# Image 0 of a four-block convolution chain: x loaded once, late weights spread over the gathers, and fewer spacer instructions between the gathers

## The reference, cut to what matters

```
L0: mid = relu(bn(conv1x1(x, 512->128)))
    offset = conv3x3(mid, 128->18)
    samp = for each of 9 taps: 4 neighbouring pixels of mid at (pixel + tap + offset),
           weighted bilinearly
    hid = relu(bn(sum over taps of conv2_w[tap] @ samp[tap]))
    x = relu(bn(conv1x1(hid, 128->512)) + x)
L1: 25 local self-correlations of x, normalised; x = relu(W @ [x, corr] + b)
L2, L3: x = relu(bn(1x1, 3x3, 1x1 bottleneck of x) + x)
```

## Time and profile before

| | |
|---|---|
| median of 3 runs | 602.6 us |
| profiled execution: its own time, its span | 605.4 us, 603.6 us |
| busy: TensorE, VectorE, ScalarE, GpSimd | 562.2, 442.3, 327.3, 409.5 us |
| first gather of image 0, of image 1, last of image 3 | 24.9, 129.2, 471.7 us |
| moved by DMA | 110.1 MB |

### The profile page before, as it was taken

The page is one execution under the profiler, slowest core; times in us unless marked ns, Lnnn a source line. Parts: engine busy times, 40 slices in busy tenths (PEclk is TensorE's granted clock), DMA queues, the critical chain, the costliest instruction groups (busy, mean ns, idle before and its releaser), DMA issues.

```text
span 603.6 us, 8850 instructions
## 1 busy us (share of the span) xinstructions
PE 562.2 (93%) x2550; PEld 416.9 (69%) x2550; DVE 442.3 (73%) x1277; ACT 327.3 (54%) x718; POOL 409.5 (68%) x718
## 2 busy tenths in 40 slices
PE   9478986699999999799999999999999999999996
PEld 4434753576777777469777777688777776987774
DVE  3447789798988788689986788998884674463444
ACT  3445756446654874555645857654557633433534
POOL 2388888888888898888888888888787300003060
PEclk9888998899999999899999999999999999999999
DMA  8898997964568555866586557856765213000003
GB/s 307 286 355 292 276 366 222 310 186 143 160 193 296 165 150 162 280 205 171 168 264 204 168 168 251 251 159 175 223 183 148 72 59 134 0 1 1 1 1 139
DMA packets 48034, 110.08 MB, mean 182 GB/s; under 512 B 7655, under 2 KB 15911, under 8 KB 47858
## 3 DMA queue, kind: packets, MB, share of 16 engines
q0 software_dynamic: 23040, 75.52, 41.8%
q1 hardware_dynamic: 22274, 32.59, 15.6%
q10 hardware_dynamic: 2672, 1.41, 0.8%
HBM read 96.94 MB, written 12.55 MB: 181 GB/s over the span
## 4 chain that ended last, share of the span: by engine, by line
PE 71%; POOL 18%; DVE 4%; issue 3%; DMA 2%; ACT 1%; POOLq 0%; DVEq 0%; ACTq 0%
PE bank L630 16%; PE bank L632 16%; PE bank L631 16%; POOL patch L597 14%; PE bank L741 7%; POOL tick L602 4%; PE bank L749 4%; PE bank L818 4%; PE bank L730 4%; DMA patch<-patch_tables,idx_all 2%; PE bank L787 1%; PE bank L666 1%; PE bank L653 1%; DVE samp L1189 1%; DVE ring L1250 1%
## 5 line engine op out<-in xcount | busy, mean ns | idle before, releaser
L1189 DVE SCALAR_TENSOR_TENSOR samp<-patch,wgt_all,samp 128x128 f32<-128x128 f32 x864 | 240.7, 347 | 22.7 <-ACT samp L911 20.1
L597 POOL DMA_INDIRECT patch<-patch_tables,idx_all x216 | 219.8, 1017 | 40.2 <-DVE samp L1189 10.7
L911 ACT ACTIVATE samp<-patch,wgt_all 128x128 f32<-128x128 f32 x288 | 102.0, 396 | 76.4 <-DMA patch<-patch_table,idx_all 35.3
L597 POOL DMA_INDIRECT patch<-patch_table,idx_all x72 | 70.5, 980 | 30.9 <-DVE far L1086 20.3
L613 POOL TENSOR_TENSOR kept<-xs_high,xs_low 128x512 f32<-128x512 f32 x12 | 16.5, 1405 | 100.3 <-PE bank L632 100.3
L602 POOL TENSOR_TENSOR tick<-tick 1x1 f32<-1x1 f32 x288 | 79.7, 277 | 5.0
L741 PE MATMUL bank<-sampT,w 128*128 128x512 f32 x144 | 71.9, 606 | 1.5 <-ACT sampT L919 1.5
L730 PEld LDWEIGHTS bank<-ident_r,samp 128*128 128x128 f32 x288 | 35.8, 144 | 31.4 <-DVE samp L1189 16.8
L919 ACT ACTIVATE sampT<-bank 128x512 f32<-128x512 f32 x72 | 41.9, 591 | 27.8 <-PE bank L730 26.8
L730 PE MATMUL bank<-ident_r,samp 128*128 128x128 f32 x288 | 44.1, 280 | 10.5 <-DVE samp L1189 10.5
L630 PE MATMUL bank<-x_high,l1w_high 128*128 128x512 f32 x128 | 53.9, 421 | 0.0
(11 more groups left out here) (187 smaller groups left out, 1203.1 us busy)
## 6 DMA issues: line engine op xcount, KB each, us to landing
x_whole<-in_x SPq DMA_DIRECT2D x32, 256.0 KB, 7.2
out_y<-ring SPq DMA_DIRECT2D x32, 256.0 KB, 3.3
xa<-in_x SPq DMA_DIRECT2D x6, 1024.0 KB, 8.5
patch<-patch_tables,idx_all POOLq DMA_INDIRECT x216, 3.5
patch_tables<-midT SPq DMA_DIRECT2D x11, 256.0 KB, 7.1
xa<-in_x SPq DMA_DIRECT2D x8, 256.0 KB, 5.7
patch<-patch_table,idx_all POOLq DMA_INDIRECT x72, 6.0
l1w_whole<-in_l1wt SPq DMA_DIRECT2D x1, 1024.0 KB, 10.4
```

The source lines that it names most:

```text
L597: pool.indirect_dma_start(patch[:, n % SLOTS].rearrange("p a c -> p (a c)"), None, patches_n if i else patches_0, bass.IndirectOffsetOnAxi ...
L911: act.activation(samp[:, n % SAMPS, t, :], patch[:, g % SLOTS, 0, :], ACT.Copy, scale=wgt_all[:, i, (HT * h + t) * TAPS + k, 0:1]).then_in ...
L1189: dve.scalar_tensor_tensor(o_, g_, w_, o_, ALU.mult, ALU.add).then_inc(blended, 1)
```

## The change

The list is planned anew: all engines' items stand in another order (the bulk of the diff, not shown). What was counted in it for this document stands in the prediction. Nine items are gone (`xload.1.0` and all eight `res.0`), ten `ldw` items (loads of weights) are new. The code outside the list:

```diff
-PAUSE, PAUSES = 120, 2
+PAUSE, PAUSES = 120, (0, 1, 2, 2)
+WEIGHT_PACE = {7: 1, 2: 2, 3: 2, 4: 3, 5: 3, 0: 4, 1: 4, 6: 7}
+X_PACE = {2: 0, 3: 5}
...
             def load_x(i, h):
-                sp.dma_start(xa[:, :, h * HALF:(h + 1) * HALF],
-                             x_v[i, :, :, h * HALF:(h + 1) * HALF]).then_inc(ld_xa[h], 16)
-
+                some = slice(h * KC // 2, (h + 1) * KC // 2)
+                sp.dma_start(xa[:, some, :], x_v[i, :, some, :]).then_inc(ld_xa[h], 16)
+
+            for k in range(KC):
+                sp.dma_start(whole["x1"][:, k, PADK:PADK + H, :], grid_rows(x_v[0, :, k, :])).then_inc(ld_x0[k], 16)
             for h in range(2):
-                for k in range(KC):
-                    cols = slice(h * HALF, (h + 1) * HALF)
-                    sp.dma_start(xa[:, k, cols], x_v[0, :, k, cols]).then_inc(ld_x0[h][k], 16)
-            for n in (2, 3, 4, 5, 6, 0, 1):
...
-            sp.wait_ge(tabled[0], table_dmas(0))
-            sp.wait_ge(conv1_done, nth(("conv1", 0, 1)))
-            load_x(1, 1)
...
+                load_x(1, h)
 
             for it in ORDER:
                 if it[0] == "xload":
                     _, i, h = it
-                    sp.wait_ge(conv1_done, nth(("conv1", i - 1, h)))
+                    sp.wait_ge(conv1_done, nth(("conv1", i - 1, 0), ("conv1", i - 1, 1)))
+                    sp.wait_ge(turned, nth(("turn", 0, X_PACE[i] + h)))
                     load_x(i, h)
+                elif it[0] == "ldw":
+                    n = it[1]
+                    if n in WEIGHT_PACE:
+                        sp.wait_ge(turned, nth(("turn", 0, WEIGHT_PACE[n])))
+                    else:
+                        sp.wait_ge(tabled[0], table_dmas(0))
...
                                 .then_inc(gathered[n % SLOTS], 16)
+                        if i == 0 and t % 2 == 0:
+                            continue
                         pool.wait_ge(ticked, ticks[0] + 1)
                         pool.tensor_tensor(tick[:, 1:2], tick[:, 0:1], tick[:, 0:1], ALU.add).then_inc(ticked, 1)
                         ticks[0] += 1
-                        for _ in range(PAUSES if i and t == HT - 1 else 0):
+                        for _ in range(PAUSES[i] if t == HT - 1 else 0):
...
-            for _ in range(3):
-                pe.matmul(bank[TURN_BANK][:], w3_s[:, 0:P], w3_s[:], start=True, stop=True)
-            pe.wait_ge(ld_first, 32)
+            for n in (C, C // 2):
+                pe.matmul(bank[TURN_BANK][:, 0:n], w3_s[:, 0:P], w3_s[:, 0:n], start=True, stop=True)
+            pe.wait_ge(ld_w1, 16)
...
+                        elif h == 0:
+                            pe.wait_ge(ld_x0[c], 16)
+                            for half in range(2 if c < KC - 1 else 1):
+                                last = pe.matmul(first[half][:], w1[:, c, :], residual(half, c),
+                                                 start=c == 0, stop=c == KC - 1)
```

More of the change, by code:

```diff
@@ L50 @@
[L50 to L74, removed]
@@ new lines @@
+weigh.0.4.0 tap.0.1 turn.0.3 ldw.4 gather.0.5.1 conv1.2.1 midT.1.0 ldw.5 weigh.0.4.1 blend.0.4.0 gather.0.6.0
+blend.0.4.1 conv1.2.0 hats.1 gather.0.6.1 weigh.0.5.0 blend.0.5.0 weigh.0.5.1 gather.0.7.0 sampT.0.3 mid.2.1 turn.0.4
+midT.2.1 split.3 weigh.0.6.0 blend.0.5.1 positions.1 splitlow.3 ldw.0 gather.0.7.1 ldw.1 weigh.0.6.1 mid.2.0
+pixels.1.0 blend.0.6.0 turn.0.5 tap.0.2 tap.0.3 midT.2.0 split.5 blend.0.6.1 gather.0.8.0 xload.3.0 pixels.2.0
+weigh.0.7.0 taps.2.1 tapped.2.1 sampT.0.4 weigh.0.7.1 sampT.0.5 gather.0.8.1 splitlow.5 blend.0.7.0 blend.0.7.1
@@ new lines @@
+gather.0.12.1 blend.0.11.0 hid.0.0 weigh.0.11.1 split.4 out0.0.0.0 out0.0.0.2 gather.0.13.0 out0.0.0.3 splitlow.1
+blend.0.11.1 gather.0.13.1 split.6 sampT.0.9 weigh.0.12.0 turn.0.10 out0.0.0.1 turn.0.11 xsum.0.0.2 blend.0.12.0
+conv1.3.1 weigh.0.12.1 xhigh.0.0.2 mid.3.0 gather.0.14.0 xsum.0.0.1 weigh.0.13.0 gather.0.14.1 xhigh.0.0.1 corrw
+xsum.0.0.3 splitlow.4 gather.0.15.0 xhigh.0.0.3 sampT.0.11 xsum.0.0.0 xlow.0.0.2 blend.0.12.1 xlow.0.0.1 blend.0.13.0
+mid.3.1 weigh.0.13.1 weigh.0.14.0 sampT.0.10 tap.0.9 tap.0.10 turn.0.12 midT.3.1 taps.3.0 gather.0.15.1 weigh.0.14.1
@@ new lines @@
+turn.0.16 sampT.0.15 blend.0.17.1 sampT.0.16 gather.1.1.0 weigh.1.0.0 turn.0.17 tap.0.15 sampT.0.17 tap.0.16
+gather.1.1.1 tap.0.17 splitlow.6 index.3 hid.0.1 weigh.1.0.1 gather.1.2.0 blend.1.0.0 out0.0.1.2 out0.0.1.3
+blend.1.0.1 out0.0.1.0 out0.0.1.1 gather.1.2.1 turn.1.0 xsum.0.1.2 hats.3 positions.3 xsum.0.1.3 xhigh.0.1.2
+weigh.1.1.0 weigh.1.1.1 xhigh.0.1.3 gather.1.3.0 xlow.0.1.2 xsum.0.1.1 xsum.0.1.0 xhigh.0.1.1 mixA.0.0.0 mixA.0.0.1
+xlow.0.1.3 xhigh.0.1.0 weigh.1.2.0 xlow.0.1.1 borders xlow.0.1.0 blend.1.1.0 gram.0.1 gather.1.3.1 weigh.1.2.1
@@ new lines @@
+weigh.3.3.1 hid.2.1 xsum.2.0.1 blend.3.3.0 gather.3.5.1 turn.3.2 turn.3.1 final.1.1.1 xhigh.2.0.1 sampT.3.2
+blend.3.3.1 store.1.1.1 weigh.3.4.0 xlow.2.0.1 out0.2.1.3 out0.2.1.0 gather.3.6.0 blend.3.4.0 sampT.3.1 weigh.3.4.1
+tap.3.0 out0.2.1.1 mixA.2.0.0 tap.3.1 tap.3.2 out0.2.1.2 blend.3.4.1 gather.3.6.1 turn.3.3 xsum.2.1.1 xsum.2.1.3
+xsum.2.1.0 xhigh.2.1.3 xhigh.2.1.0 xlow.2.1.3 turn.3.4 gram.2.0 xlow.2.1.0 gather.3.7.0 xsum.2.1.2 weigh.3.5.0
+xhigh.2.1.1 xhigh.2.1.2 weigh.3.5.1 xlow.2.1.1 weigh.3.6.0 xlow.2.1.2 gather.3.7.1 blend.3.5.0 gram.2.1 copies.2.0
```

365 lines of the change are left out of this document (186 added, 179 removed).

## The result

The changed kernel takes **610.4 us** in the median of 4 runs (608.6 to 611.1), the kernel before on the same chip 603.0 (602.5 to 605.9): a ratio of **1.0116, 95% interval 1.0081 to 1.0151**. The forecast was 597.6 with a range of 590.5 to 604.5. It is slower, by 7.4 us, where a gain of 5 was foreseen. The profiled execution of the change (608.6) is its fastest, that of the kernel before (605.4) one of its slower ones, so the two traces lie only 3.2 us apart in span; they show how the parts moved, the ratios say how much it came to.

What follows compares the result with a forecast made beforehand. The prediction saw a start, a stretch at POOL's pace (image 0's gathers), then one at TensorE's. Its terms, -1.0 - 11.7 + 1 + 5.7 + 3 - 2 = -5.0, took 602.6 to 597.6 us, range 590.5 to 604.5.

Steps and rivals of the forecast that it cites:

- Term 1: First stage: halved warm-up and no parameter wait bring the first gather earlier, -1.0 us (bounds -2.5 to +1.0).
- Term 2: POOL in image 0: 36 dropped ticks save 0.325 us a pair, -11.7 us.
- rival B: POOL in image 0: a gather directly behind a gather pays what the tick paid; 608.3 us, chance 0.15.
- Term 3: Faster stretch at POOL's pace: VectorE, TensorE and DMA nearly full, so lumps cost +1 us (0 to +6).
- rival D: First stretch: VectorE or transfers full, POOL waits for slots, half the tick gain lost; 602.3 us, chance 0.20.
- Term 4: TensorE: two mixA move behind image 0's last tap, 2.85 us each, +5.7 us.
- term 5: VectorE behind image 0's last blend: splitlow.6, index.3, positions.3 delay xsum and xlow for gram, +3 us (0 to +6.2).
- term 6: TensorE's wait at 230 to 260 us for image 1's last gathers shrinks, -2 us (0 to -4.2).

Runs made afterwards that it cites:

- u3_pause: The change with two memsets per four gathers in image 1 again, not one; 614.17 us, ratio 1.0167.
- v1_rest: Kernel before, its list and early weights kept, with most other edits of the change (ticks, single x load, halved warm-up, conv1's start, pauses); 596.65 us, ratio 0.9878.
- d1_ticks: Kernel before without the tick behind the first gather of each pair of image 0; 602.67 us, ratio 0.9988.
- d2_xonce: Kernel before with image 0's x loaded once, into the residual's place, in the same eight pieces; 603.10 us, ratio 0.9993.
- d3_noticks: Kernel before with no tick at all in image 0; 598.67 us, ratio 0.9910.
- o2_mixA: The change with index.3, hats.3, positions.3, borders, splitlow.6 and two mixA moved back near their old places in its list; 616.74 us, ratio 1.0219.
- o1_borders: The change with index.3, hats.3, positions.3 and borders moved up in its list; 654.6 us, ratio 1.0439, on a slower chip.
- u2b_ticks: The change with a tick again behind every gather of image 0; 610.98 us, ratio 1.0113.
- h3_mixA: v1_rest with two mixA moved behind tap.0.17, image 0's last tap; 652.4 us, ratio 1.0342, on a slower chip.

## Why the prediction was wrong

**Term 1, the first gather, -1.0 (bounds -2.5 to +1.0).** Measured +0.8 in the change's trace and -2.1 in u3_pause's, from the same code; v1_rest, with the same warm-up, lies between (conv1's 14 pieces in 7.40, the first gather at 23.82). In two microseconds of that stretch, the change and u3_pause:
```profile
9.00:11.00 2.00, 2.00 (x4) 0.74 (x3) 1.21 (x7) 0.23 (x2) 0.00 (x0) 1.00 1.02 418
```
```profile
9.00:11.00 2.00, 2.00 (x6) 0.85 (x5) 1.21 (x7) 0.21 (x2) 0.00 (x0) 1.00 1.02 420
```
TensorE is busy throughout in both, with four pieces begun in the one and six in the other, and the granted clock reads 1.00, the level of 2.4 GHz, in both. It reads 1.00 from 1.47 to 5.00 in the trace of before too, where the warm-up's pieces take 0.92 us each and conv1's later 0.47, so at the start of the kernel this column does not tell the two paces apart. The bounds held; the single value hid that the outcome varies. What decides it stays open.

**Term 2, the ticks, -11.7.** This is the step that failed: "if the second gather starts 0.01 behind the first as the tick does now". It starts 0.30 behind. The tick's 0.18 and 0.16 are exchanged for a gap of 0.30, so a pair saves 0.06 us and not 0.325, 2.2 us over 36 pairs, and d1_ticks shows that even this does not arrive. It is rival B's mechanism, just short of its bound: by B there is nothing to win from a second gather of 1.30 us on, and it takes 1.24, 0.30 to start and 0.94. B's "against", that each tick starts at once behind its gather, was no evidence on a gather; the idle 0.16 behind each tick should have told me that a gather has a start of its own to pay.

The sum's other half, that the excess over the shortest step is inherited and not saved, was right in kind; its size varies. Over the 71 steps it is 9.4 us before, 12 us in d1_ticks, 7.6 us in the change's trace (mean step less half of the shortest pair, times 71). It stands beside VectorE's subtractions of two SBUF operands. In the change a tick lasts 2.12 us from 131.11 on, beside `splitlow.6`:
```profile
131.11 2.12 POOL L613 TENSOR_TENSOR tick<-tick 1x1 f32<-1x1 f32 x1
```
```profile
130.90 2.28 DVE L1185 TENSOR_TENSOR l1w_low<-l1w_whole,l1w_high 128x2048 fp32r<-128x2048 f32 x1
```
In v1_rest it is a second gather itself, with no tick ahead of it, that lasts 2.54 where others last 0.95, beside two such subtractions:
```profile
47.09 2.54 POOL L596 DMA_INDIRECT patch<-patch_table,idx_all  x1 [0.30 <-issue]
```
```profile
46.86 1.35 DVE L1175 TENSOR_TENSOR l2w_low<-l2w_whole,l2w_high 128x1152 fp32r<-128x1152 f32 x1
48.12 0.68 DVE L1175 TENSOR_TENSOR l3w_low<-l3w_whole,l3w_high 128x512 fp32r<-128x512 f32 x1
```
The Trainium skill's rule on two SBUF inputs (SBUF — State Buffer, Who interferes with whom) had been set against the change in just this form, and this trace agrees with it for the gather too: the gather begins 0.23 us after the first subtraction and ends 0.83 us after the second. The same section infers that such a subtraction does not hold up the writing of a transfer's descriptors; the 2.54 us of this indirect transfer speak against that. In the prediction's own pair the agreement is less clean than it says: the tick begins at 78.47, 0.05 ahead of the subtraction, so by the starts it was the earlier one that waited.

**Term 3, +1.** The stretch at POOL's pace got 3.9 us shorter, where terms 2 and 3 together said 10.7. In image 0 POOL does not wait for slots; rival D did not happen. The bytes were right: 282 GB/s in 108.6 us are 30.6 MB, 30.1 had been worked out, though the text says half of image 1's x where its 2.1 MB are the whole.

**Term 4, two `mixA`, +5.7.** The work behind the last tap grew by 5.0 us and 24 pieces: right in the two traces, with the 2 us of doubt on the trace of before (against d1_ticks, d2_xonce, d3_noticks and v1_rest it is 6.6 to 7.5). o2_mixA shows that its reverse is not a gain: with this work, and VectorE's of term 5, ahead of the last tap in this list, the tap comes later by more than the work behind it falls.

**Terms 5 and 6, +3 and -2.** Together +1.0; the idle time behind the last tap grew by 1.3. The agreement is luck in part. The wait in 230 to 260, 4.2 us before, is gone, as term 6 said with its bound. Up to 170 us the idle time grew by 3.1, the size of term 5 but not its mechanism: TensorE waits 1.8 us for `corr` and 1.5 for `gs` there, and never for the `xlow` that term 5 named (in o2_mixA it does, 3.4 us). Behind 500 us it grew by 1.5, for which no term stood. ScalarE's copies into `corr` waited 2.6 us for `borders`, costed at nothing because it still stands once in POOL's queue: I had looked at the queue it is in and not at who waits for it. How much of the 1.8 us that is stays open; moving `borders` up brought nothing in o1_borders (a slower chip) or o2_mixA, both with other moves. The pauses, costed at nothing as well, cost by the centres half a per cent for one memset in image 1 (u3_pause).

**The frame of the sum.** "The end is the time of image 0's last tap, plus the TensorE work that is left then, plus the 12.3 us that TensorE idles behind it" counts every microsecond of terms 1 to 3 in full, with the idle time fixed. That failed too. In the table above the idle time is 16.5 and 17.0 us behind the two earliest last taps of the change's list and 13.6 and 14.6 behind the two later ones, and u2b_ticks, with a last gather 2.3 us later, has the change's own ratio. So even the 10.7 us of terms 2 and 3 might not have come out at the end; no run had such a gain.

**The sum.** Between the two traces it is +3.2 and not -5.0. Of these 8.2 us, 1.8 are term 1, 6.8 terms 2 and 3, -0.7 term 4 and 0.3 terms 5 and 6. Between the medians the miss is 12.8 us (610.4 against 597.6), and the further 4.6 no trace shows. Over the runs the forecast divides thus: all but the list was to gain 13.7 us (terms 1, 2, 3 and 6), and v1_rest, which has most of it, gained 7.4 by its ratio (0.0122 x 603.7); the list was to cost 8.7 (terms 4 and 5) and cost, with the loads and what v1_rest lacks, some 14. Each side is short by about 6 us, both to the slow side. In size, 4.4 of the 11.2 us between the traces of v1_rest and the change are the waits for `corr` and `gs`, and 5.7 are two `mixA`; that these are also causes was not shown: the run that moves `mixA` alone, h3_mixA, fell on a slower chip. In which part of the list the 2.4% lie, or whether some of it lies in the edits that v1_rest lacks, stays open.

## What to carry to other kernels

An instruction that vanishes from a queue gives back its time only if the next one could have started then: look for the start-up gap of the successor's kind, and where no row shows that kind directly behind its own, take the gap behind the small instruction as part of the successor. Where a change brings new mechanisms and a new order of the work together, run the mechanisms under the old order first; here, on one chip, they win 1.2% and the order with its late loads loses 2.4%. A stretch that gets shorter is not yet time won: look at several traces whether the idle time behind it takes the gain. An item that moves in a list is to be costed by who waits for it, not by whether its own queue has room.

## What the runs showed that was not expected

- An indirect transfer directly behind another one on POOL starts 0.30 us after its end (0.16 behind a tick). At the shortest, a row of gathers with no tick runs at 1.25 us a step against 1.31 with ticks, and a pair with one tick at 1.27 and 1.30; the means over image 0 are 1.411 and 1.443.
- The same first stage gives conv1's first 14 pieces in 6.3 to 9.2 us from one execution to the next, and a first gather at 22.8 to 25.7; with the full warm-up in the changed kernel it was at 23.98 and 23.96 in two. The first stage of the kernel before varies as well: 24.94, 24.88 and 24.06 with the same code.
- An earlier last tap of image 0 did not bring an earlier end in the traces with the change's list: from 136.0 to 131.0 us, the spans stay between 606.8 and 609.7. Each of these kernels has an edit of its own, so the rule is shown for them together and not for one.
- On some chips engines wait up to 10 us at a time for nothing that the profile shows, which costs the kernel before 2 to 4% and most of the kernels made from it or from the change more.
